# Token forms of later sequences made from untransposed rows in staging, and turned by transposing transfers

## Chip, cores and metric

The kernel runs on one core of one Trainium2 chip. The metric is the device time of the whole kernel in microseconds. Before the change it is 2253.17 us, the median of 3 runs (2252.21 to 2253.98).

## The reference

The input x holds 8 sequences of 1024 tokens with 512 features. With LN a layer norm without scale, the reference computes

```
x = x + attn(LN(x))        # per sequence: latent projections, causal softmax over 1024 tokens, head size 64
h = silu(y @ W1.T) * (y @ W3.T)          # y = LN(x), W1 and W3 are 2048 x 512
x = x + (fwht(h) / sqrt(2048)) @ W2.T    # Walsh-Hadamard transform of h, W2 is 512 x 2048
```

The two products with W1 and W3 need y with its features on the partitions; the layer norm gives y with its tokens on them. So y must be turned somewhere. What changes is how it is turned, and when.

## The kernel before, in words

**The work.** A block k (`NK` = 128 of them) is one group of 128 hidden rows (h = k mod 16) of one sequence (s = k // 16). It has seven products with f16 operands, `product(k, i)` for i = 0 to 6 (line 782), in a fast scheme with 7 block products in place of 8: each is 2 x 3 matmuls of 128x512 (lines 772 to 774; high*high, high*low, low*high parts). Their results stand in the four PSUM banks `PF`. Behind products 1, 3, 5 and 6 stands `down` (lines 796 to 798), six matmuls each, which multiplies earlier blocks' hidden values by W2. A block so has 66 matmuls of 128x512.

**The tokens' forms.** `XF` holds the right operands of the seven products: 7 forms, each a high and a low f16 part of 128x1024. Some forms are quarters of the tokens' matrix y^T (in `XS`, f32), some are sums that `tokens_sum` (VectorE, line 1721) writes over quarters in `XS`. `tokens_high` (ScalarE, line 1122) rounds a form to f16 into `XF`, and `tokens_low` (VectorE, line 1711) writes the rest. Form i of the next sequence can only be written once product i of the last block of this one (h = 15) has read the old form.

**The attention of the next sequence beside it.** While sequence s is in its blocks, the attention of sequence s+1 is computed in two halves of 512 tokens (a = 2s+2 and 2s+3). Its steps hang on slots: the position f = 7h + i, with i the product, gives slot f - 3 for the first half (f - 4 when s = 0) and 42 less (`ODD`) for the second; `slots` computes it, and there were 59 (`NSLOT`). Each engine walks the same positions in its own program order, in `fill(k, i)` on ScalarE and VectorE, so one table by hand sets the order in every queue. Where an engine reaches position f early or late relative to TensorE depends on its own queue. At the end of a half VectorE does `norm2` and `norm2_root` and then `xnorm` for four tiles (line 1533): it writes a normalised 128x512 tile into the one buffer `xs`. TensorE turns it (`xtrans`, line 616: four f32 transposes of 128x128 into the PSUM half `Y`), and ScalarE copies `Y` into `XS` (line 1003).

**ScalarE's and VectorE's part in a block.** After product 0 ScalarE's `copy_b` (line 1129) copies one PSUM bank to another, and product 2 waits for it. `copy_b` itself stands behind `high(k - 1)` (line 1148) in ScalarE's queue, which waits for VectorE's `hidden(k - 1, 0)` (line 1743). After product 2 VectorE's `sum_c` (line 1729) gives the bank that product 4 waits for. ScalarE's `silu` (line 1140) follows products 3 and 5; VectorE's `hidden(k, 1)` follows the second, then `out_rows` (line 1762). At the change of a sequence the steps of the forms stand between these.

**Transfers.** All are issued by SyncE, in program order: the weights' forms `WS` for two blocks ahead (896 KB, line 408), W2 (line 419), x and xT, the output, and, in the attention, the transposing transfers of the probabilities `PT<-Ph` and `PT<-Pl` (line 431; f16, in 128x128 blocks, up to 8 blocks each).

Of the kernel before, what the change touches and what calls it, by code (L numbers as in the profile page):

```python
# [9 lines left out]
F16 = mybir.dt.float16  # L10
# [7 lines left out]
NS = 8  # L18
# [26 lines left out]
NSLOT = 59  # L45
# [56 lines left out]
def xf_no(s, i):  # L102

    return 7 * s + ((0, 2, 4, 1, 3, 5, 6)[i] if s == 0 else i) + 1

# [31 lines left out]
def build_kernel(nc, x, xT, w13, w13t, w2, small, cst, tab, wscr, w2scr, w2tmp, out):  # L137
    with ExitStack() as ctx:
# [149 lines left out]
        def xblock(i):  # L288

            half, k = XPLACE[i]  # L290
            return XS[:, half, 2 * k:2 * k + 2, :].rearrange("p k c -> p (k c)")
# [16 lines left out]
        d_raw, d_PT = sem("d_raw"), sem("d_PT")  # L308
        d_wst, d_wld, d_w2st, d_w2ld = ([sem(f"{m}{i}") for i in range(2)] for m in ("d_wst", "d_wld", "d_w2st", "d_w2ld"))
# [31 lines left out]
        def _(sp):  # L341
# [140 lines left out]
            for k in range(NK):  # L482
                s, h = divmod(k, NH)
                for j in range(7):
                    if s + 1 < NS:
                        for c, slot in slots(s, 7 * h + j):
                            attention(2 * s + 2 + c, slot)
                    if s and j == 0 and 1 <= h <= 4:
# [25 lines left out]
        def _(pe):  # L514
# [96 lines left out]
            def xtrans(a, t):  # L611
                nonlocal yfree
                w.wait_ge(v_xs, tile_no(a, t))
                w.wait_ge(*yfree)
                for j in range(4):
                    i = pe.transpose(Y[:, j * 128:(j + 1) * 128], xs[:, j * 128:(j + 1) * 128], idn)  # L616
                i.then_inc(p_xt, 1)
                yfree = (a_xn, tile_no(a, t))

            def attention(a, slot):  # L620
                if 1 <= slot <= 4:
                    cproj(a, slot - 1)
                if slot == 6:
                    latent(a)
                if slot == 13:
                    values(a)
                if slot == 14:
                    proj(a)
                for t in range(4):
                    at = slot - tile_slot(a, t)  # L630
# [6 lines left out]
                    if slot == end_slot(a) + 5 + t:  # L637
                        xtrans(a, t)
# [106 lines left out]
            def product(k, i):  # L745
# [4 lines left out]
                if h == 0:  # L750
# [176 lines left out]
        def _(ac):  # L927
# [18 lines left out]
            def latent(a):  # L946
                w.wait_ge(p_cp, tile_no(a, 3))
                if a > 1:
                    w.wait_ge(v_pl, group_no(a - 1, 3, groups(a - 1) - 1))
                ac.activation(work(a)[2], banks(a)[0], ACT.Copy).then_inc(a_cT, 1)  # L950
# [48 lines left out]
            def xtrans(a, t):  # L999
                w.wait_ge(p_xt, tile_no(a, t))  # L1000
                if a >= 2:
                    w.wait_ge(v_xf, 7 * (a // 2))
                ac.activation(XS[:, a % 2, :, t * 128:(t + 1) * 128], Y.rearrange("p (j c) -> p j c", j=4), ACT.Copy).then_inc(a_xn, 1)

            def attention(a, slot):
# [11 lines left out]
                for t in range(4):  # L1017
# [5 lines left out]
                    if slot == end_slot(a) + 5 + t:  # L1023
                        xtrans(a, t)
# [86 lines left out]
            def tokens_high(s, i):  # L1111
                if i in (0, 3):
                    w.wait_ge(a_xn, tile_no(2 * s, 3))
                elif i == 5:
                    w.wait_ge(a_xn, tile_no(2 * s + 1, 3))
                else:
                    w.wait_ge(v_t, 4 * s + {1: 1, 4: 2, 2: 3, 6: 4}[i])
                if s:
                    w.wait_ge(p_gu, gu_no(NH * s - 1, i))
                else:  # L1120
                    w.wait_ge(a_nm, 2 * NH)
                ac.activation(XF[:, 0, i, :], xblock(i), ACT.Copy).then_inc(a_xf, 1)
# [166 lines left out]
            def fill(k, j):  # L1289
# [7 lines left out]
                if s == 0 and f in SPLIT_AT:  # L1297
                    split2(SPLIT_AT[f])

            for k in range(NK):  # L1300
                s, h = divmod(k, NH)
                first, last = s > 0 and h == 0, s + 1 < NS and h == NH - 1
# [9 lines left out]
                if first:  # L1312
                    tokens_high(s, 3)
                if last:
                    tokens_high(s + 1, 0)
# [4 lines left out]
                if first:  # L1320
                    tokens_high(s, 4)
# [3 lines left out]
                if last:  # L1325
                    tokens_high(s + 1, 1)
                fill(k, 2)
                if first:
                    tokens_high(s, 5)
# [4 lines left out]
                if first:  # L1334
                    tokens_high(s, 6)
                fill(k, 4)
                silu(k, 1)
                if last:
                    tokens_high(s + 1, 2)
# [7 lines left out]
        def _(ve):  # L1347
# [166 lines left out]
            def norm2(a):  # L1514
                sv.after(kept["x2"])
                if a == 1:
                    w.wait_ge(v_xs, 4)
# [12 lines left out]
            def xnorm(a, t):  # L1530
                sv.after(kept["norm2"])
                w.wait_ge(p_xt, tile_no(a, t) - 1)
                ve.tensor_scalar(xs[:, :], xrow(a, t), st[:, 184 + 2 * t:185 + 2 * t], st[:, 84 + t:85 + t],  # L1533
# [4 lines left out]
            def attention(a, slot):  # L1538
# [25 lines left out]
                for t in range(4):  # L1564
# [9 lines left out]
                    if slot == end_slot(a) + 4 + t:  # L1574
# [134 lines left out]
            def tokens_low(s, i):  # L1709
                w.wait_ge(a_xf, xf_no(s, i))  # L1710
                ve.tensor_tensor(XF[:, 1, i, :], xblock(i), XF[:, 0, i, :], ALU.subtract).then_inc(v_xf, 1)

            def tokens_sum(s, i):

                w.wait_ge(a_xn, tile_no(2 * s + 1, 3))
# [3 lines left out]
                b12, b22 = (XS[:, 1, 2 * j:2 * j + 2, :].rearrange("p k c -> p (k c)") for j in range(2))  # L1719
                u, v = {1: (b12, xblock(0)), 4: (b22, b12), 2: (b22, xblock(1)), 6: (xblock(3), xblock(2))}[i]  # L1720
                ve.tensor_tensor(xblock(i), u, v, ALU.subtract).then_inc(v_t, 1)
# [168 lines left out]
            def fill(k, j):  # L1890
# [5 lines left out]
                if s == 0:  # L1896
# [5 lines left out]
                    if f in SPLIT_AT:  # L1902
                        split2(SPLIT_AT[f])

            for k in range(NK):
                s, h = divmod(k, NH)
                first, last = s > 0 and h == 0, s + 1 < NS and h == NH - 1
# [5 lines left out]
                if first:  # L1913
                    tokens_low(s, 3)
                    tokens_low(s, 4)
                fill(k, 0)
                if last:
                    tokens_low(s + 1, 0)
                    tokens_sum(s + 1, 1)
# [8 lines left out]
                if first:  # L1928
                    tokens_low(s, 5)
                    tokens_sum(s, 6)  # L1930
                if last:
                    tokens_low(s + 1, 1)
                    tokens_sum(s + 1, 4)
# [3 lines left out]
                if k == 0 or first:  # L1937
                    tokens_low(s, 6)
                if last:
                    tokens_sum(s + 1, 2)  # L1940
# [3 lines left out]
                if last:  # L1944
                    tokens_low(s + 1, 2)
# [129 lines left out]
```

## Time and profile before

| | |
|---|---|
| median of 3 runs | 2253.17 us |
| the profiled execution's own time | 2254.15 us |
| its span (first to last instruction) | 2252.3 us |
| mean granted TensorE clock | 0.983 of full speed |
| TensorE matmul busy | 2143.6 us (95%) |
| VectorE, ScalarE, GpSimd busy | 64%, 44%, 10% of the span |

In the profile a matmul's record is longer than its share of the array, because matmuls overlap: one of 128x512 is recorded with 0.38 us while the next starts 0.216 us after it. So the distance between starts tells what an instruction costs TensorE. "Idle before" counts from the recorded end, and is 0.16 us less than what the array lost.

### The profile page before, as it was taken

To read this page: it belongs to the slowest core of one execution; us is meant where nothing else is said; L and a number is where in the kernel's file an instruction comes from. 1 tells how busy PE (TensorE), PEld (TensorE's weight loads), DVE (VectorE), ACT (ScalarE), POOL (GpSimd) and SP (SyncE) were. 2 spreads that over 40 slices of the span, in tenths; PEclk is the share of its full clock that TensorE was granted. 3 is DMA by queue.
4 is the path that set the end of the run, shared out by engine and by line. 5 is a ranking of instruction groups with operands and counts; after the bars stand their busy time and mean duration, and the time that the engine had idled before them with its cause. 6 is when DMAs were issued, how large, how long until landed. Compare 5 with 4: busy or idle time off the path is not lost. (4 is left out here: it accounts for less than half of the span.)

```text
span 2252.3 us, 27382 instructions
## 1 busy us (share of the span) xinstructions
PE 2143.6 (95%) x10108; PEld 1012.6 (45%) x10108; DVE 1448.9 (64%) x2758; ACT 982.7 (44%) x1493; POOL 234.1 (10%) x212
## 2 busy tenths in 40 slices
PE   6778899999999999999999999999999999999999
PEld 3433444444444444444444444444444444444444
DVE  7886676767657675666757675576756667563333
ACT  6855454434443534434444444435344344442221
POOL 2344554000000000000000000000000000000000
PEclk8789999999999999999999999999999999999999
DMA  8344324333233323234233332333332342323221
GB/s 330 138 146 156 123 93 130 122 108 103 91 97 120 120 101 99 88 114 140 74 107 116 116 98 87 102 115 121 100 99 94 111 137 74 105 82 112 84 85 54
DMA packets 127654, 252.97 MB, mean 112 GB/s; under 512 B 74528, under 2 KB 74656, under 8 KB 122144
## 3 DMA queue, kind: packets, MB, share of 16 engines
q1 hardware_dynamic: 127520, 251.21, 33.7%
q8 instruction: 81, 1.33, 0.2%
q14 instruction: 53, 0.43, 0.1%
HBM read 194.81 MB, written 39.85 MB: 104 GB/s over the span
## 5 line engine op out<-in xcount | busy, mean ns | idle before, releaser
L772 PE MATMUL PF<-XF,WS 128*128 128x512 f16 x1792 | 685.4, 382 | 17.8 <-ACT PF L1129 10.0
L773 PE MATMUL PF<-XF,WS 128*128 128x512 f16 x1792 | 683.1, 381 | 0.0
L774 PE MATMUL PF<-XF,WS 128*128 128x512 f16 x1792 | 682.8, 381 | 0.0
L796 PE MATMUL PD<-W2S,H 128*128 128x512 f16 x1024 | 388.6, 379 | 0.0
L797 PE MATMUL PD<-W2S,H 128*128 128x512 f16 x1024 | 388.6, 379 | 0.0
L798 PE MATMUL PD<-W2S,H 128*128 128x512 f16 x1024 | 388.6, 379 | 0.0
L1140 ACT ACTIVATE SH<-PF,afs 128x512 f32<-128x512 f32 x256 | 175.8, 687 | 378.6 <-PE PF L774 377.8
L772 PEld LDWEIGHTS PF<-XF,WS 128*128 128x128 f16 x1792 | 176.1, 98 | 245.9 <-issue 39.1
L1743 DVE SCALAR_TENSOR_TENSOR SH<-PF,afs,SH 128x512 f32<-128x512 f32 x256 | 191.8, 749 | 140.3 <-ACT SH L1140 118.1
L1148 ACT ACTIVATE H<-SH 128x1024 f16<-128x1024 f32 x128 | 135.2, 1056 | 323.9 <-DVE SH L1743 323.9
L774 PEld LDWEIGHTS PF<-XF,WS 128*128 128x128 f16 x1792 | 176.2, 98 | 214.1 <-issue 4.7
L773 PEld LDWEIGHTS PF<-XF,WS 128*128 128x128 f16 x1792 | 176.4, 98 | 179.2 <-issue 8.0
L1751 DVE TENSOR_TENSOR H<-SH,H 128x1024 f16<-128x1024 f32 x128 | 156.8, 1225 | 130.3 <-ACT H L1148 130.1
L1762 DVE SCALAR_TENSOR_TENSOR ring<-PD,afs,ring 128x512 f32<-128x512 f32 x224 | 166.8, 745 | 52.5 <-PE PD L798 52.0
L1964 POOL TENSOR_TENSOR ring<-ring,bb 128x512 f32<-128x512 f32 x56 | 70.9, 1289 | 1231.6 <-DVE st L1388 1211.7
L1733 DVE TENSOR_TENSOR PF<-PF,p 128x512 f32<-128x512 f32 x128 | 89.1, 696 | 130.6 <-PE PF L774 129.7
L796 PEld LDWEIGHTS PD<-W2S,H 128*128 128x128 f16 x1024 | 100.3, 98 | 121.2 <-issue 0.6
L798 PEld LDWEIGHTS PD<-W2S,H 128*128 128x128 f16 x1024 | 100.3, 98 | 121.2 <-issue 0.6
L797 PEld LDWEIGHTS PD<-W2S,H 128*128 128x128 f16 x1024 | 100.3, 98 | 121.1 <-issue 0.6
L1729 DVE TENSOR_TENSOR PF<-PF,p 128x512 f32<-128x512 f32 x128 | 88.8, 693 | 20.0 <-PE PF L774 18.5
L1134 ACT ACTIVATE p<-PF 128x512 f32<-128x512 f32 x128 | 75.1, 587 | 36.9 <-PE PF L774 36.9
L1129 ACT ACTIVATE PF<-PF 128x512 f32<-128x512 f32 x128 | 74.4, 581 | 26.4 <-PE PF L774 26.4
(310 smaller groups left out, 2195.8 us busy)
## 6 DMA issues: line engine op xcount, KB each, us to landing
WS<-wscr SPq DMA_DIRECT2D x112, 896.0 KB, 4.7
W2S<-w2scr SPq DMA_DIRECT2D x30, 1024.0 KB, 4.8
xraw<-xT SPq DMA_DIRECT2D x58, 256.0 KB, 3.5
ring<-x SPq DMA_DIRECT2D x56, 256.0 KB, 4.3
wscr<-WS SPq DMA_DIRECT2D x16, 896.0 KB, 4.2
out<-ring SPq DMA_DIRECT2D x56, 256.0 KB, 2.9
XF<-w SPq DMA_DIRECT2D x16, 512.0 KB, 7.5
RAW<-w13t SPq DMA_DIRECT2D x16, 512.0 KB, 4.1
```

The costliest lines, as they stand in the source:

```text
L772: pe.matmul(bank, wh, th, start=i < 2 and j == 0, stop=False, skip_group_check=True)
L773: pe.matmul(bank, wh, tl, start=False, stop=False, skip_group_check=True)
L774: m = pe.matmul(bank, wl, th, start=False, stop=j == 1, skip_group_check=True)
L796: pe.matmul(PD[:, t % 2, :], th, wh, start=j == 0, stop=False)
L797: pe.matmul(PD[:, t % 2, :], th, wl, start=False, stop=False)
L798: m = pe.matmul(PD[:, t % 2, :], tl, wh, start=False, stop=j == 3)
L1140: ac.activation(SH[:, i, :], PF[:, (1 - k % 2, 2)[i], :], ACT.Silu, scale=afs[:, k % NH:k % NH + 1]).then_inc((a_sb, a_sc2)[i], 1)
L1148: ac.activation(H[:, q % 2, k % 4, 0, :], SH[:, :, :].rearrange("p i c -> p (i c)"), ACT.Copy).then_inc(a_hi, 1)
L1733: ve.tensor_tensor(PF[:, 3, :], PF[:, k % 2, :], p5[:, :], ALU.add).then_inc(v_e, 1)
L1743: ve.scalar_tensor_tensor(SH[:, i, :], PF[:, (k % 2, 3)[i], :], afs[:, 16 + h:17 + h], SH[:, i, :], ALU.mult, ALU.mult).then_inc((v_hA, v_ ...
L1751: ve.tensor_tensor(H[:, q % 2, k % 4, 1, :], SH[:, :, :].rearrange("p i c -> p (i c)"), H[:, q % 2, k % 4, 0, :], ALU.subtract).then_inc(v ...
L1762: ve.scalar_tensor_tensor(row, PD[:, t % 2, :], afs[:, 65:66], row, ALU.mult, ALU.add).then_inc(v_ev, 1)
```

## The change

From the second sequence on, `xnorm` writes its rows straight into `XS`, tokens on the partitions, one slot earlier. Sums and the f16 split work on these rows as they lie. The split goes to staging: three pairs of buffers in turn (form i uses pair i mod 3), which the attention has done with by then, `Ph`/`Pl`, `PT` and `PB`. SyncE's new `load_form` turns each part with one transposing transfer of 8 blocks into `XF`: 14 of them per sequence. TensorE's `xtrans`, ScalarE's copy out of `Y`, and the slots for them are gone. The forms' steps now have positions of their own, f = 96 to 111 of sequence s and 0 to 2 of the next. Within a form the columns now lie as (tile, half, 128) in place of (half, tile, 128), so that a matmul's moving operand is four pieces of 128 columns, 256 columns apart. The first sequence keeps its transposes and takes the new layout.

```
-NSLOT = 59
+NSLOT = 57
+def xload_no(s, i):
+    return 32 * ((3, 2, 2)[i % 3] * (s - 1) + i // 3 + 1)
...
+        def staging(i, m):
+            return ((Ph[:, :], Pl[:, :]), (PT[:, 0, :], PT[:, 1, :]),
+                    tuple(PB[:, h * 512:(h + 1) * 512].bitcast(F16) for h in range(2)))[i % 3][m]
...
+            def load_form(s, i):
+                w.wait_ge(p_gu, gu_no(NH * s - 1, i))
+                w.wait_ge(a_xf, xf_no(s, i))
+                for m in range(2):
+                    if m:
+                        w.wait_ge(v_xf, xf_no(s, i))
+                    sp.dma_start_transpose(XF[:, m, i, :].rearrange("p (b c) -> p b c", c=128), staging(i, m)).then_inc(d_XF[i % 3], 16)
...
# SyncE, s + 1 < NS: load_form(s + 1, i) at f == 105, 106, 108, 110, 111 for i = 0 to 4
# SyncE, s > 0:      load_form(s, 5) at f == 0, load_form(s, 6) at f == 2
...
# TensorE: def xtrans and its call are removed; product(k, i) with h == 0:
+                if h == 0 and s == 0:
                     w.wait_ge(v_xf, xf_no(s, i))
+                elif h == 0:
+                    w.wait_ge(d_XF[i % 3], xload_no(s, i))
-                    th, tl = (XF[:, m, i, j * 512:(j + 1) * 512] for m in range(2))
+                    th, tl = (XF[:, m, i, :].rearrange("p (t f c) -> p t f c", t=4, f=2)[:, j] for m in range(2))
...
# ScalarE: def xtrans and its call are removed; latent(a) waits, for even a > 2, also for
+                    w.wait_ge(p_gu, gu_no(NH * (a // 2 - 1), 6))
# tokens_high(s, i), in place of the wait for product i of the last block:
+                elif i >= 3:
+                    w.wait_ge(d_XF[i % 3], xload_no(s, i - 3))
+                elif i == 0:
+                    w.wait_ge(d_PT, pt_no(2 * s + 1, 3))
+                elif i == 1:
+                    w.wait_ge(p_pv, group_no(2 * s + 1, 3, 1))
+                else:
+                    w.wait_ge(v_pl, group_no(2 * s + 1, 3, 1))
# ScalarE's positions, s + 1 < NS: tokens_high(s + 1, i) at f == 96, 103, 105, 108, 109, 111
#   for i = 0 to 5 (before: i = 0, 1, 2 at h == 15); s > 0: tokens_high(s, 6) at f == 1
#   (before: i = 3, 4, 5, 6 at h == 0)
...
# VectorE: norm2(a) waits for v_xs 4 * a; xnorm(a, t) at end_slot(a) + 3 + t (before + 4 + t):
-                w.wait_ge(p_xt, tile_no(a, t) - 1)
-                ve.tensor_scalar(xs[:, :], xrow(a, t), ...
+                w.wait_ge(v_xf, 7 * (a // 2))
+                ve.tensor_scalar(XS[:, a % 2, t, :], xrow(a, t), ...
# VectorE's positions, s + 1 < NS: f == 97 low 0; 102 sum 1; 103 sum 4; 104 low 1 and sum 2;
#   106 low 2; 109 low 3; 110 low 4 and sum 6; s > 0: f == 0 low 5; 2 low 6
#   (before: low 0, sum 1, low 1, sum 4, sum 2, low 2 at h == 15; low 3, low 4, low 5, sum 6, low 6 at h == 0)
```

The lines that begin with # sum up lines of the diff in words.

## Rows read from the trace of the kernel before

**Rows 1.** The page: busy time, and TensorE's granted clock in 40 slices.
```profile
PE 2143.6 (95%) x10108; PEld 1012.6 (45%) x10108; DVE 1448.9 (64%) x2758; ACT 982.7 (44%) x1493; POOL 234.1 (10%) x212
PEclk8789999999999999999999999999999999999999
```
**Rows 2.** Busy time per engine in two stretches: sequence 2's blocks, sequence 7's last ones.
```profile
688.00:949.80 261.80, 257.11 (x1242) 121.65 (x1241) 171.93 (x334) 113.86 (x167) 9.98 (x8) 1.00 0.33 106
1998.90:2241.00 242.10, 242.10 (x1123) 109.65 (x1122) 99.33 (x124) 62.62 (x85) 0.00 (x0) 1.00 0.26 88
```
**Rows 3.** Timeline, TensorE, second tile turned without a wait: start, recorded us, instruction.
```profile
549.48 0.38 PE L798 MATMUL PD<-W2S,H 128*128 128x512 f16 x1
549.69 0.60 PE L616 MATMUL XY<-cst_s,xs 128*128 128x128 f32 x4
550.13 0.38 PE L772 MATMUL PF<-XF,WS 128*128 128x512 f16 x1
```
**Rows 4.** Waits of TensorE from 426 to 1999 us: total, times, longest.
```profile
PE XY L616 <- DVE xs L1533: 4.7, 12, 0.6
```
**Rows 5.** Timeline, TensorE, position 4 of sequence 2: the first projection of the attention.
```profile
696.85 0.38 PE L774 MATMUL PF<-XF,WS 128*128 128x512 f16 x1
697.90 0.50 PE L529 MATMUL XY<-Kh,Wc 128*128 128x512 f32 x1 [0.68 <-DVE Kl L1383]
```
**Rows 6.** Timeline, VectorE, what stands ahead of that projection's low part.
```profile
694.90 1.22 DVE L1711 TENSOR_TENSOR XF<-XS,XF 128x1024 f16<-128x1024 f32 x1
696.03 1.22 DVE L1721 TENSOR_TENSOR XS<-XS 128x1024 f32<-128x1024 f32 x1
697.16 0.69 DVE L1383 TENSOR_TENSOR Kl<-xraw,Kh 128x512 fp32r<-128x512 f32 x1
```
**Rows 7.** Timeline, TensorE, the first sequence's blocks: two tiles turned after waits.
```profile
287.27 0.63 PE L616 MATMUL XY<-cst_s,xs 128*128 128x128 f32 x4 [1.43 <-ACT XS L1003]
...
402.06 0.66 PE L616 MATMUL XY<-cst_s,xs 128*128 128x128 f32 x4 [1.95 <-DVE xs L1533]
```
**Rows 8.** Groups by line and form: count, busy us, mean ns, idle before.
```profile
L1140 ACT ACTIVATE SH<-PF,afs 128x512 f32<-128x512 f32 x235 | 161.4, 687 | 350.7 <-PE PF L774 349.9
L1743 DVE SCALAR_TENSOR_TENSOR SH<-PF,afs,SH 128x512 f32<-128x512 f32 x236 | 176.8, 749 | 132.7 <-ACT SH L1140 111.9 <-PE PF L774 20.4
L1148 ACT ACTIVATE H<-SH 128x1024 f16<-128x1024 f32 x118 | 124.7, 1056 | 297.8 <-DVE SH L1743 297.8
L1762 DVE SCALAR_TENSOR_TENSOR ring<-PD,afs,ring 128x512 f32<-128x512 f32 x203 | 151.1, 744 | 33.1 <-PE PD L798 32.6
L1122 ACT ACTIVATE XF<-XS 128x1024 f16<-128x1024 f32 x49 | 50.8, 1052 | 25.5 <-DVE XS L1721 25.5
L1003 ACT ACTIVATE XS<-XY 128x512 f32<-128x512 f32 x52 | 30.9, 595 | 62.1 <-PE XY L616 62.1
```
**Rows 9.** Timeline around block 30 (h = 14): ScalarE's `copy_b`, then TensorE's product 2.
```profile
660.82 0.58 ACT L1129 ACTIVATE PF<-PF 128x512 f32<-128x512 f32 x1
...
661.64 0.38 PE L772 MATMUL PF<-XF,WS 128*128 128x512 f16 x1
```
**Rows 10.** Transfers by issue: count, median us to landing; one late issue of 8 blocks; landing range.
```profile
PT<-Ph SPq DMA_TRANSPOSE x56, 2.7
PT<-Pl SPq DMA_TRANSPOSE x56, 2.6
...
906.52 1.33 SPq L431 DMA_TRANSPOSE PT<-Pl  x1
...
DMA to landing us min/median/max: 2.3/2.6/4.5
```
**Rows 11.** Timeline, TensorE: eight f16 matmuls of 128 columns, and the next product.
```profile
531.13 0.61 PE L597 MATMUL XY<-PT,V 128*128 128x128 f16 x8
531.58 0.38 PE L772 MATMUL PF<-XF,WS 128*128 128x512 f16 x1
```

More of the change, by code:

```diff
@@ L286, in xrow, with xquarter, xblock, xpart @@
             return ring[:, r, :] if r < 16 else WX[:, t * 512:(t + 1) * 512]
-        def xblock(i):
-            half, k = XPLACE[i]
-            return XS[:, half, 2 * k:2 * k + 2, :].rearrange("p k c -> p (k c)")
+        def xquarter(s, half, k):
+            if s == 0:
+                return XS[:, half, 2 * k:2 * k + 2, :].rearrange("p f (t c) -> p f t c", t=4)
+            return XS[:, half, :, k * 256:(k + 1) * 256]
+        def xblock(s, i):
+            return xquarter(s, *XPLACE[i])
+        def xpart(s, i, m):
+            if s == 0:
+                return XF[:, m, i, :].rearrange("p (t f c) -> p f t c", t=4, f=2)
+            return staging(i, m).rearrange("p (t c) -> p t c", t=4)
+        def staging(i, m):
+            return ((Ph[:, :], Pl[:, :]), (PT[:, 0, :], PT[:, 1, :]),
+                    tuple(PB[:, h * 512:(h + 1) * 512].bitcast(F16) for h in range(2)))[i % 3][m]
         def parts_taken(a, t):
@@ L308, in build_kernel @@
         d_raw, d_PT = sem("d_raw"), sem("d_PT")
+        d_XF = [sem(f"d_XF{i}") for i in range(3)]
         d_wst, d_wld, d_w2st, d_w2ld = ([sem(f"{m}{i}") for i in range(2)] for m in ("d_wst", "d_wld", "d_w2st", "d_w2ld"))
@@ L487, in _ @@
                             attention(2 * s + 2 + c, slot)
+                    f = 7 * h + j
+                    if s + 1 < NS:
+                        if f == 105:
+                            load_form(s + 1, 0)
+                        if f == 106:
+                            load_form(s + 1, 1)
+                        if f == 108:
+                            load_form(s + 1, 2)
+                        if f == 110:
+                            load_form(s + 1, 3)
+                        if f == 111:
+                            load_form(s + 1, 4)
+                    if s:
+                        if f == 0:
+                            load_form(s, 5)
+                        if f == 2:
+                            load_form(s, 6)
                     if s and j == 0 and 1 <= h <= 4:
@@ L609, in outp @@
                 yfree = (v_x2, tile_no(a, t))
[L611 to L618, printed above, removed]
             def attention(a, slot):
@@ L636, in attention @@
                         outp(a, t)
-                    if slot == end_slot(a) + 5 + t:
-                        xtrans(a, t)
             def scores1(a, t):
@@ L770, in product @@
                     wh, wl = (WS[:, k % 2, m, WFORM[i], j * 128:(j + 1) * 128] for m in range(2))
-                    th, tl = (XF[:, m, i, j * 512:(j + 1) * 512] for m in range(2))
+                    th, tl = (XF[:, m, i, :].rearrange("p (t f c) -> p f t c", t=4, f=2)[:, j] for m in range(2))
                     pe.matmul(bank, wh, th, start=i < 2 and j == 0, stop=False, skip_group_check=True)
@@ L949, in latent @@
                     w.wait_ge(v_pl, group_no(a - 1, 3, groups(a - 1) - 1))
+                if a > 2 and a % 2 == 0:
+                    w.wait_ge(p_gu, gu_no(NH * (a // 2 - 1), 6))
                 ac.activation(work(a)[2], banks(a)[0], ACT.Copy).then_inc(a_cT, 1)
@@ L997, in parts_o @@
                 ac.activation(l[0:64, :], h[0:64, :].bitcast(F32), ACT.Copy).then_inc(a_ol, 1)
[L999 to L1003, printed above, removed]
             def attention(a, slot):
@@ L1022, in attention @@
                         parts_o(a, t, oh, ol)
-                    if slot == end_slot(a) + 5 + t:
-                        xtrans(a, t)
             def norms(h, i):
@@ L1111, in tokens_high @@
             def tokens_high(s, i):
+                rows = v_xs if s else a_xn
                 if i in (0, 3):
-                    w.wait_ge(a_xn, tile_no(2 * s, 3))
+                    w.wait_ge(rows, tile_no(2 * s, 3))
                 elif i == 5:
-                    w.wait_ge(a_xn, tile_no(2 * s + 1, 3))
+                    w.wait_ge(rows, tile_no(2 * s + 1, 3))
                 else:
                     w.wait_ge(v_t, 4 * s + {1: 1, 4: 2, 2: 3, 6: 4}[i])
-                if s:
-                    w.wait_ge(p_gu, gu_no(NH * s - 1, i))
-                else:
-                    w.wait_ge(a_nm, 2 * NH)
-                ac.activation(XF[:, 0, i, :], xblock(i), ACT.Copy).then_inc(a_xf, 1)
+                if s == 0:
+                    w.wait_ge(a_nm, 2 * NH)
+                elif i >= 3:
[4 more added lines that the diff above has]
+                    w.wait_ge(p_pv, group_no(2 * s + 1, 3, 1))
+                else:
+                    w.wait_ge(v_pl, group_no(2 * s + 1, 3, 1))
+                ac.activation(xpart(s, i, 0), xblock(s, i), ACT.Copy).then_inc(a_xf, 1)
             def copy_b(k):
@@ L1298, in fill @@
                     split2(SPLIT_AT[f])
+                if s + 1 < NS:
+                    if f == 96:
+                        tokens_high(s + 1, 0)
+                    if f == 103:
+                        tokens_high(s + 1, 1)
+                    if f == 105:
+                        tokens_high(s + 1, 2)
+                    if f == 108:
+                        tokens_high(s + 1, 3)
+                    if f == 109:
+                        tokens_high(s + 1, 4)
+                    if f == 111:
+                        tokens_high(s + 1, 5)
+                if s and f == 1:
+                    tokens_high(s, 6)
             for k in range(NK):
                 s, h = divmod(k, NH)
-                first, last = s > 0 and h == 0, s + 1 < NS and h == NH - 1
                 split = s == 0 and 1 <= h < NH - 1
@@ L1311, in _ @@
                         tokens_high(0, i)
[L1312 to L1315, printed above, removed]
                 if split:
@@ L1319, in _ @@
                 copy_p5(k)
-                if first:
-                    tokens_high(s, 4)
                 if split:
@@ L1324, in _ @@
                 fill(k, 1)
-                if last:
-                    tokens_high(s + 1, 1)
                 fill(k, 2)
-                if first:
-                    tokens_high(s, 5)
                 silu(k, 0)
@@ L1333, in _ @@
                 fill(k, 3)
-                if first:
-                    tokens_high(s, 6)
                 fill(k, 4)
                 silu(k, 1)
-                if last:
-                    tokens_high(s + 1, 2)
                 fill(k, 5)
@@ L1515, in norm2 @@
                 sv.after(kept["x2"])
-                if a == 1:
-                    w.wait_ge(v_xs, 4)
+                if a:
+                    w.wait_ge(v_xs, 4 * a)
                 for t in range(4):
@@ L1531, in xnorm @@
                 sv.after(kept["norm2"])
-                w.wait_ge(p_xt, tile_no(a, t) - 1)
-                ve.tensor_scalar(xs[:, :], xrow(a, t), st[:, 184 + 2 * t:185 + 2 * t], st[:, 84 + t:85 + t],
+                w.wait_ge(v_xf, 7 * (a // 2))
+                ve.tensor_scalar(XS[:, a % 2, t, :], xrow(a, t), st[:, 184 + 2 * t:185 + 2 * t], st[:, 84 + t:85 + t],
                                  ALU.subtract, ALU.mult).then_inc(v_xs, 1)
@@ L1573, in attention @@
                         parts_o(a, t, X[:, 0:128], oh, ol)
-                    if slot == end_slot(a) + 4 + t:
+                    if slot == end_slot(a) + 3 + t:
                         xnorm(a, t)
@@ L1710, in tokens_low @@
                 w.wait_ge(a_xf, xf_no(s, i))
-                ve.tensor_tensor(XF[:, 1, i, :], xblock(i), XF[:, 0, i, :], ALU.subtract).then_inc(v_xf, 1)
+                ve.tensor_tensor(xpart(s, i, 1), xblock(s, i), xpart(s, i, 0), ALU.subtract).then_inc(v_xf, 1)
             def tokens_sum(s, i):
-                w.wait_ge(a_xn, tile_no(2 * s + 1, 3))
+                w.wait_ge(v_xs if s else a_xn, tile_no(2 * s + 1, 3))
                 w.wait_ge(v_t, 4 * s + {1: 0, 4: 1, 2: 2, 6: 3}[i])
                 w.wait_ge(v_xf, xf_no(s, {1: 0, 4: 0, 2: 1, 6: 3}[i]))
-                b12, b22 = (XS[:, 1, 2 * j:2 * j + 2, :].rearrange("p k c -> p (k c)") for j in range(2))
-                u, v = {1: (b12, xblock(0)), 4: (b22, b12), 2: (b22, xblock(1)), 6: (xblock(3), xblock(2))}[i]
-                ve.tensor_tensor(xblock(i), u, v, ALU.subtract).then_inc(v_t, 1)
+                b12, b22 = xquarter(s, 1, 0), xquarter(s, 1, 1)
+                u, v = {1: (b12, xblock(s, 0)), 4: (b22, b12), 2: (b22, xblock(s, 1)), 6: (xblock(s, 3), xblock(s, 2))}[i]
+                ve.tensor_tensor(xblock(s, i), u, v, ALU.subtract).then_inc(v_t, 1)
             def sum_c(k):
@@ L1903, in fill @@
                         split2(SPLIT_AT[f])
+                if s + 1 < NS:
+                    if f == 97:
+                        tokens_low(s + 1, 0)
+                    if f == 102:
+                        tokens_sum(s + 1, 1)
+                    if f == 103:
+                        tokens_sum(s + 1, 4)
+                    if f == 104:
+                        tokens_low(s + 1, 1)
+                        tokens_sum(s + 1, 2)
+                    if f == 106:
+                        tokens_low(s + 1, 2)
+                    if f == 109:
+                        tokens_low(s + 1, 3)
+                    if f == 110:
+                        tokens_low(s + 1, 4)
+                        tokens_sum(s + 1, 6)
+                if s:
+                    if f == 0:
+                        tokens_low(s, 5)
+                    if f == 2:
+                        tokens_low(s, 6)
             for k in range(NK):
                 s, h = divmod(k, NH)
-                first, last = s > 0 and h == 0, s + 1 < NS and h == NH - 1
                 if k:
@@ L1912, in _ @@
                     low_part(k - 1)
-                if first:
-                    tokens_low(s, 3)
-                    tokens_low(s, 4)
                 fill(k, 0)
-                if last:
-                    tokens_low(s + 1, 0)
-                    tokens_sum(s + 1, 1)
                 fill(k, 1)
@@ L1927, in _ @@
                     tokens_sum(0, 6)
[L1928 to L1933, printed above, removed]
                 fill(k, 2)
@@ L1936, in _ @@
                 sum_e(k)
-                if k == 0 or first:
+                if k == 0:
                     tokens_low(s, 6)
-                if last:
-                    tokens_sum(s + 1, 2)
                 fill(k, 4)
@@ L1943, in _ @@
                 out_rows(k // 4 - 1, 2 * (k % 4))
-                if last:
-                    tokens_low(s + 1, 2)
                 fill(k, 5)
```

1 line of the change is left out of this document (removed).

## The prediction

> **What bounds the kernel now.** I read the page first. TensorE is recorded busy for 95% of the span, and from the third slice of 40 on its granted clock is near full (2.4 GHz) [rows 1]. Then two stretches: in a sequence with attention beside it (261.8 us) TensorE is busy for 257.1, VectorE for 172, ScalarE for 114; in the last sequence, without attention, TensorE is busy without a gap [rows 2]. So TensorE's queue is the bound, and a change is worth what it takes from or adds to that queue: instructions at their distance from start to start, and gaps. VectorE and ScalarE count only where they are late for TensorE. Third, the waits tell which gaps belong to what is removed [rows 4 to 7].
>
> **The change part by part.** Seven sequences get new forms this way, 14 halves of four tiles: 56 groups of four f32 transposes.
>
> *Removed, TensorE's transposes.* Between two products a group takes the place from 549.69 to 550.13: 0.44 us [rows 3]. 56 x 0.44 = **24.6 us**, all of it in the queue that binds.
>
> *Removed, the waits ahead of them.* `xs` is a single buffer: VectorE can write the next tile only when the last is turned. In the sequences 1 to 6 TensorE waits 12 times for it, 4.7 us recorded [rows 4], and 0.16 us more each time, since a record outlasts its share of the array (0.38 against 0.22): 4.7 + 12 x 0.16 = **6.6 us**. In the first sequence there are two larger ones, 1.43 and 1.95 recorded [rows 7]. The first waits for ScalarE's copy out of `Y`, which goes: 1.6 us. The second stands where VectorE is late with everything, and whoever waits for it next (product 4, for `sum_c`, ahead of which a form's low part and two tiles now stand) loses about as much. I take **1.6** of both, with 0 and 5 as ends.
>
> *Removed, ScalarE's copies.* 56 x 0.595 = 33 us [rows 8], off TensorE's path, taken at nothing: ScalarE is busy for 44%. If its cover went, it would be a gain.
>
> *Moved, the forms' steps.* Their number and size are as before. Ahead of the first projection at position 4, VectorE now works through five forms' steps after the change of sequence (low 3, 4, 5, sum 6, low 6), the last two before the low part of xT for which TensorE waits [rows 6]; the gap is 697.90 - 696.85 - 0.22 = 0.83 us [rows 5]. After the change only low 5 and low 6 stand there, two operations of 1.22 in place of four or five, so this gap goes: 6 x 0.83 = **5.0 us** (the seventh change of sequence is followed by no attention).
>
> They move to the last three blocks, and there they delay `copy_b`, for which product 2 waits. Three places, by the durations of [rows 8]:
> - End of h = 13: low 0 (1.22; its successor starts 1.14 later [rows 6]) stands ahead of `hidden`, behind which stand `high` and `copy_b` on ScalarE. `copy_b` ends at 661.40 now, and product 2 starts at 661.64 [rows 9]: 0.24 of slack, so 0.9 us of new gap.
> - End of h = 14: after the second silu VectorE does `hidden` 0.75, `out_rows` 0.74, sum 4, low 1 and sum 2 (1.22 each, [rows 6, 8]), `hidden` 0.75; then ScalarE `high` 1.06 and `copy_b` 0.58. That is 7.54, plus silu's 0.69 and some 0.2 to start it, less about 0.5 since VectorE's operations overlap by 0.08: 7.9 us after the end of product 5. TensorE reaches the next product 2 after six groups of six matmuls, 36 x 0.216 = 7.8. New gap some 0.3.
> - End of h = 15: the same with low 4 and sum 6 only, but `tokens_high` 5 (1.05) ahead of `copy_b`: 7.4 + 0.9 - 0.4 = 7.9. New gap some 0.3.
>
> Together 1.5 us, seven times: **10.5 us** given back. Ends: 0 (the gaps merge, since each one gives VectorE time) and 3 us each, 21, if starts and semaphores add up.
>
> *Added, 98 transposing transfers* (14 x 7), on SyncE's queue. The trace has 112 of their kind. A late one of 8 blocks, the same 256 KB, holds SyncE 1.33 us; to landing it is 2.3 to 4.5 us from the issue [rows 10]. Two of a pair are issued 1.3 us apart and each lands 2.6 or 2.7 after its own issue, so they overlap. Per sequence SyncE spends 14 x 1.3 = 18 us on them, in a stretch of some 25. The tightest is form 5: its low part ends after hidden, `high`, low_part and itself, some 6.2 us after product 6 of h = 15; issue and landing (3 to 4) make 9 to 10; product 5 of the new sequence starts eight groups of six (10.4), the last gap (0.3) and a projection (0.6) later, at about 11.3. Slack 1 us or more, so nothing. Form 6 has 2 us, forms 0 to 4 more. Behind these transfers stand, on SyncE, the weights for h = 1 (1.5 us later, needed 14 us on), W2 (needed four blocks on), and xT: hidden. If a landing took 2 us more, form 5 would be late by 1.
>
> *Added waits.* ScalarE's for the staging buffers: forms 3 and 4 need loads 0 and 1, issued behind products 0 and 1, 4 us and more earlier; behind them in the queue stand the second silu and `copy_b`. `latent`'s wait is for a product three positions back. VectorE's `norm2` waits for its own past work. Nothing for each; GpSimd's queue is not touched.
>
> *Changed, the moving operand.* All 5376 matmuls of products now read four pieces of 128 columns. No row shows such an operand. Lower end 0; upper end: each piece as dear as a matmul of its own, 0.45 us for eight [rows 11], 0.056 each, 4 x 0.056 - 0.216 = 8 ns, or 45 us. I take 0, since the nearest row is the product's own matmul of 512 columns, of which only the addresses change, while the upper end counts four instructions where there is one. The Trainium skill (SBUF — State Buffer, "Door 1: The DMA port swizzle", the note on "cachelines") ties the penalty for a stride to how many accesses in a row fall into one 16-byte line. Within a piece the elements stay dense, so by it the cost would be 0; no run here shows it.
>
> **Sum.** 24.6 + 6.6 + 1.6 + 5.0 - 10.5 = 27.3. From the profiled execution's 2254.15 that is 2226.9; the median of the runs is 1 us below that execution, so **2226 us**. With the terms' ends: 24.6 + 6.6 + 5 + 5.0 = 41 at best (2212), 24.6 + 6.6 + 0 - 21 = 10 at worst (2243).
>
> **The rivals.**
> 1. *Strided operand dear.* Place: every product's matmul; price up to 8 ns each, 45 us. The time would be 2226 + 45 = 2271, slower. It decides from 27.3 / 5376 = 5 ns on. Against it: the operand's data are as dense within a piece as before. Chance 0.04.
> 2. *Forms land late.* Rows as above say no. But take the parts one after another, each with its 3.2 us to landing: 14 x 3.2 = 45 us from the end of product 0 of h = 15, where the need of the last is some 27 us on. Then 18 us of gap per change of sequence, 7 x 18 = 126, about 2352. The Trainium skill (VectorE: DVE Perf Modes, "The three transpose paths" and "Rules for kernel authors") speaks against this change: it gives 390 ns for a 128x128 transpose on TensorE and 1309 ns for one by DMA, and says to use TensorE where a PSUM destination is fine. By its figure 14 x 8 x 1.3 would be an estimated 147 us per sequence, far more. The trace disagrees, with 8 blocks issued in 1.33 us and landed within 4.5 [rows 10]. A partial lateness of 4 us at each change would cancel the gain. Chance 0.06.
> 3. *Only the exchange of waits differs.* `copy_b`'s gaps stay away, and the gain is the removed terms: 36 to 41 us, 2212 to 2217. For it: 90 us of idle VectorE time in a sequence [rows 2]. Chance 0.18.
> 4. *The chain behind `copy_b` grows*, 3 us or more per change, with the gap at position 4 still there: 5 to 14 us gained, 2239 to 2248. Chance 0.12.
> 5. *Nothing to be seen.* The transposes filled time that other waits take over. Against it: 42 of 56 groups have no wait ahead of them. Chance 0.04.
>
> **How the numbers follow.** The forecast, 2218 to 2238, has 0.56. A measurement of this kernel can tell 0.2% (4.5 us) from no change. Faster by more: the forecast, rival 3, rival 4: 0.86; within: rival 5, 0.04; slower: rivals 1 and 2, 0.10. The range takes in the forecast, rival 3 and the nearer part of rival 4: 2212 to 2241.
>
> **What would show it.** No L616 and no ScalarE copy out of `XY` after the first blocks; a sequence 3.5 us shorter for the transposes, with the `xs` waits gone. At h = 14, h = 15 and the next h = 0, gaps of product 2 on `copy_b` of 0.3 to 0.9 us. At position 4 no gap. XF<-staging transfers landing 2.5 to 4.5 us after issue, and no wait of TensorE on them. The distance of product matmuls still 0.216. The forecast is wrong if that distance grows, if TensorE waits for `XF` transfers, or if ScalarE waits for them and `copy_b` behind it.

## The result, and the profile after

The changed kernel takes 2260.3 us (median of 7 runs, 2257.8 to 2261.96) against 2253.17 us before (7 runs): ratio 1.0032, 95% interval 1.002 to 1.0043. It is slower by 7 us, where 27 us less were forecast. The profiled execution's span went from 2252.3 to 2259.3 us.

The page of the kernel after:

```profile
span 2259.3 us, 26978 instructions
PE 2132.1 (94%) x9884; PEld 986.5 (44%) x9884; DVE 1449.7 (64%) x2758; ACT 948.6 (42%) x1437; POOL 233.7 (10%) x212
PEclk8789999999999999999999999999999999999999
```

The 224 transposes are gone (10108 matmuls before [rows 1], 9884 now), and ScalarE has 34 us less to do. VectorE's work is as it was. So the removal is real, and the gain went elsewhere. Busy time in stretches of the kernel after, the first being sequence 3's blocks:

```profile
954.60:1215.60 261.00, 253.95 (x1209) 117.70 (x1208) 171.90 (x334) 108.98 (x159) 9.97 (x8) 1.00 0.41 120
1069.70:1085.30 15.60, 15.40 (x73) 7.16 (x73) 13.49 (x35) 4.93 (x8) 3.60 (x3) 1.00 0.22 83
1085.30:1102.50 17.20, 15.84 (x76) 7.21 (x75) 13.34 (x32) 5.29 (x8) 1.38 (x2) 1.00 0.32 115
```

A sequence takes 261.0 us against 261.8 [rows 2]: a gain of 0.8 where some 4 were forecast. TensorE's busy time fell by 3 us, but the idle time rose. And this sequence is one of the better ones. Both kernels have one wait of 0.47 us for `copy_b` late in each sequence; from one of these to the next it is 264.0, 261.1, 262.1, 266.7 and 261.1 us now, and was 261.8, 261.8, 262.7, 262.7 and 261.9. Who ended its gaps, from 428 to 2005 us:

```profile
PE PF L811 <- ACT PF L1170: 15.5, 30, 0.8
PE XY L577 <- DVE Kl L1424: 13.3, 18, 2.7
PE XY L601 <- DVE V L1473: 9.1, 12, 1.1
PE XY L645 <- DMA PT<-Pl: 8.9, 14, 2.5
PE PF L811 <- DVE PF L1771: 1.2, 6, 0.2
```

The first row is `copy_b` (7.5 us in 12 waits before, 15.5 in 30 now). Of the 18 new waits the prediction had 12, two at each of six changes of sequence (0.76 and 0.28); the other six, of 0.28, stand at position 57 of each sequence. No row names the forms' transfers. But the projections of an attention (L577) wait 13.3 us in place of 6.7, and up to 2.7 in place of 0.7, and `values` (L601) 9.1 in place of 2.5, with six new waits of 1.1. The prediction had neither growth. TensorE's timeline at both, and at the two larger `copy_b` gaps:

```profile
969.72 0.38 PE L837 MATMUL PD<-W2S,H 128*128 128x512 f16 x1
971.47 0.50 PE L577 MATMUL XY<-Kh,Wc 128*128 128x512 f32 x1 [1.38 <-DVE Kl L1424]
...
1090.76 0.38 PE L813 MATMUL PF<-XF,WS 128*128 128x512 f16 x1
1092.23 0.40 PE L601 MATMUL XY<-id,V 128*128 128x128 f16 x4 [1.09 <-DVE V L1473]
1092.47 0.38 PE L811 MATMUL PF<-XF,WS 128*128 128x512 f16 x1
1092.68 0.38 PE L812 MATMUL PF<-XF,WS 128*128 128x512 f16 x1
...
1190.56 0.39 PE L811 MATMUL PF<-XF,WS 128*128 128x512 f16 x1 [0.76 <-ACT PF L1170]
...
1205.26 0.39 PE L811 MATMUL PF<-XF,WS 128*128 128x512 f16 x1 [0.28 <-ACT PF L1170]
```

With the 0.16 that a record hides, the gap ahead of the projection is 1.54 us here, of `values` 1.25 and of `copy_b` 0.92 and 0.44. Product matmuls follow at 0.21 to 0.22 us as before, so the strided operand costs nothing. (The slice in the kernel is `rearrange("p (t f c) -> p f t c", t=4, f=2)[:, j]`: half j of all four tiles. The cut of the code under "The change" has `p t f c` there, which would take tile j.)

**Where xT is late.** SyncE's timeline of the kernel after, at the start of sequence 4, and then the issues of that stretch (count, KB, median us to landing):

```profile
1219.07 2.68 SPq L463 DMA_TRANSPOSE XF<-PB  x2
1221.79 1.40 SPq L463 DMA_TRANSPOSE XF<-Ph  x1
1223.23 1.34 SPq L463 DMA_TRANSPOSE XF<-Pl  x1
1224.62 0.58 SPq L441 DMA_DIRECT2D W2S<-w2scr  x1
1225.24 1.46 SPq L385 DMA_DIRECT2D xraw<-xT  x2
1226.74 2.13 SPq L380 DMA_DIRECT2D WX<-x  x4
...
W2S<-w2scr SPq DMA_DIRECT2D x1, 1024.0 KB, 5.4
xraw<-xT SPq DMA_DIRECT2D x2, 256.0 KB, 5.6
```

Before, W2 was issued 5.8 us ahead of xT and had landed by then:

```profile
1215.61 0.32 SPq L419 DMA_DIRECT2D W2S<-w2scr  x1
1221.41 2.68 SPq L363 DMA_DIRECT2D xraw<-xT  x2
```

SyncE now comes to W2's place in its program only behind `load_form` 5 and 6, which wait for VectorE. So 1 MB goes out 0.6 us ahead of xT, for which the next projections wait. In the kernel before the first xT load of a sequence landed 2.8 or 2.9 us after its issue; now the two loads behind W2 take 5.6 to 6.5 us (the median of the two, in each of the six sequences). Over all the loads that their line issues the median went from 3.5 to 5.1: minimum, median and maximum of line 385 after and of line 363 before are

```profile
DMA to landing us min/median/max: 2.9/5.1/8.1
```

```profile
DMA to landing us min/median/max: 2.8/3.5/7.8
```

The gaps behind it differ per sequence (1.5 to 2.9 us), and in two of the six TensorE's clock falls: behind those recorded with 2.69 and 1.93 us, but not behind one of 2.28. The largest:

```profile
705.74 0.38 PE L837 MATMUL PD<-W2S,H 128*128 128x512 f16 x1
708.80 0.50 PE L577 MATMUL XY<-Kh,Wc 128*128 128x512 f32 x1 [2.69 <-DVE Kl L1424]
...
712.45 0.63 PE L812 MATMUL PF<-XF,WS 128*128 128x512 f16 x1
712.88 0.63 PE L813 MATMUL PF<-XF,WS 128*128 128x512 f16 x1
```

After the gap matmuls follow at 0.43 us, the lower of the two levels (1.2 GHz), for some 3 us, which costs 1.7 more. Read off the timeline in this way, the six sequences lose about 15 us to xT: 11.9 in gaps, and twice 1.7 to the clock.

**Where VectorE is the bound.** The two blocks h = 7 and 8 together took 34.0 us before and take 32.8 now:

```profile
802.30:820.90 18.60, 17.62 (x90) 8.86 (x90) 15.14 (x40) 6.72 (x11) 4.99 (x4) 1.00 0.21 77
820.90:836.30 15.40, 15.40 (x77) 7.34 (x75) 11.54 (x27) 5.78 (x9) 0.00 (x0) 1.00 0.32 116
```

These are the rows of before, to be held against the second and third stretch after. The first block lost 3.0 us, as forecast (four groups of 0.44 and 1.1 of waits), but VectorE's work of both blocks stayed at some 26.8 us. It has hardly a gap there. Its busy time (the third engine in the row) is 17.1 of the 18.0 us from position 52 to 58 after, and was 17.0 of 19.1 before:

```profile
1074.20:1092.20 18.00, 16.67 (x79) 7.46 (x77) 17.14 (x52) 4.17 (x7) 4.99 (x4) 1.00 0.23 81
806.80:825.90 19.10, 18.32 (x95) 9.22 (x92) 16.98 (x52) 6.40 (x11) 4.99 (x4) 1.00 0.14 49
```

At position 58 TensorE needs `values`' operand, at the end of VectorE's chain for the second half (`norm1`), and it waits for `copy_b` at 57: 1.7 us come back.

### The profile page after: what moved, and what is told of

Same layout as the page of the kernel before. It is cut to its first block and busy times, and to the rows that moved or that the text cites. A ratio compares the mean times of both kernels' runs of the same rounds, so it can differ in the third digit from the quotient of the medians.

```text
span 2259.3 us, 26978 instructions
## 1 busy us (share of the span) xinstructions
PE 2132.1 (94%) x9884; PEld 986.5 (44%) x9884; DVE 1449.7 (64%) x2758; ACT 948.6 (42%) x1437; POOL 233.7 (10%) x212
```

## The experiments

The ratios are against the kernel before, measured beside each on the same chip (2252.6 to 2253.5 us). Gains over the kernel after are against its 2260.3 us, a difference of two medians.

**W2 one block later.** In the kernel after:

```
-                    if j == 2 and k % 4 == 0 and k >= 8:
+                    if k >= 8 and j == 2 and (k % NH == 1 if k % NH < 4 else k % 4 == 0):
                         load_w2s(k // 4)
```

> The kernel after, with the W2 load of a sequence's first block issued one block later (at h = 1 in place of h = 0), so that it no longer stands just ahead of the first xT loads on SyncE's queue. Theory A (the xT transfers for positions 3 and 4 land late because the 1 MB of W2 now runs ahead of them): the gap of TensorE ahead of the projection at position 7 (1.5 to 2.9 us and up to 1.7 us of half clock, 13.6 us in sequences 1 to 6) goes, xT lands 3 to 4 us after its issue again, and the time is 2246 to 2249 us, against 2260 after. Rival B (the transposing transfers themselves are what xT waits behind): xT still lands 5 us or more after its issue, the gap stays, 2258 to 2261.

Measured 2243.59 us, ratio 0.9956 (0.9942 to 0.9971). The median is 16.7 us below the kernel after, 2.4 us more than theory A's band allows. This one issue decides between slower and faster than before. TensorE's waits of this kernel, 427 to 1988 us, and its transfers:

```profile
PE XY L577 <- DVE Kl L1424: 3.2, 14, 0.6
```

```profile
xraw<-xT SPq DMA_DIRECT2D x58, 256.0 KB, 3.8
```

13.3 us became 3.2. The loads into `xraw` land in 3.8 us at the median (4.9 after, 3.5 before), and W2, now behind them, is waited for by nobody. Rival B falls: the transposing transfers still go out right ahead of xT, yet a sequence's first xT load lands after 3.3 to 3.5 us in the four sequences where it can be read alone.

**Is it the order alone?** The first attempt moved W2 in the kernel before from behind position 2 to ahead of the xT loads.

> The kernel before, unchanged but for the issue of W2 in a sequence's first block, which moves from behind position 2 to just ahead of the xT loads of position 3. Theory A (the order alone makes xT late): xT lands 5 us or more after its issue, TensorE gets a gap ahead of the projection at position 6 or 7 of 1 us and more in each of 6 sequences, 2259 to 2264 us. Rival B (the transposing transfers' own traffic is needed for it): no such gap, 2252 to 2256.

Measured 2253.16 us, ratio 1.0002 (0.9992 to 1.0011). That says nothing on the question: SyncE waits for nothing between the two places, so W2 left 5.8 us ahead of xT, as before. The second attempt holds W2 back in time:

```
+                    if h == 0 and k >= 8 and j == 3:
+                        if s + 1 < NS:
+                            w.wait_ge(v_xl, tile_no(2 * s + 2, 0))
+                        load_w2s(k // 4)
```

> The previous run of this question (e8_before_w2_at_xt) moved the issue in the program but not in time, since SyncE waits for nothing between: W2 was still issued 5.8 us ahead of xT. Here the kernel before issues W2 of a sequence's first block only after the same wait as the xT load of position 3, so right ahead of it, with no transposing transfers near. Theory A (the order alone makes xT late): xT lands 5 us or more after its issue in place of 2.9, and TensorE gets a gap of 1 us and more ahead of the projection of position 6 or 7: 2259 to 2266 us. Rival B (the transposing transfers' traffic is needed too): xT lands within 4 us, 2252 to 2256.

Measured 2260.78 us, ratio 1.0034 (1.002 to 1.0047): the order alone, without one transposing transfer of forms, makes the kernel before 8 us slower. SyncE's timeline in it, the landing of both transfers, and the waits for the projections (426 to 1999 us):

```profile
961.60 0.32 SPq L419 DMA_DIRECT2D W2S<-w2scr  x1
961.97 2.32 SPq L363 DMA_DIRECT2D xraw<-xT  x2
```

```profile
W2S<-w2scr SPq DMA_DIRECT2D x1, 1024.0 KB, 4.8
xraw<-xT SPq DMA_DIRECT2D x1, 256.0 KB, 5.3
```

```profile
PE XY L533 <- DVE Kl L1387: 11.7, 24, 1.0
```

In the six sequences this first xT load lands 5.3 to 5.6 us after its issue, as theory A has it. Six gaps of 0.84 (recorded) came on top of the 18 before, 6.0 of the 8 us. They are smaller than in the kernel after, where x and the last forms are issued in the same few microseconds too; how much of the rest is those transfers was not tried.

**Transposes put back where VectorE is busy.** In the kernel after, at the first half's old places:

```
+            def turn_nothing(a, t):
+                w.wait_ge(*yfree)
+                for j in range(4):
+                    pe.transpose(Y[:, j * 128:(j + 1) * 128], idn, idn)
...
+                    if a % 2 == 0 and slot == end_slot(a) + 5 + t:
+                        turn_nothing(a, t)
```

> The kernel after, with four f32 transposes of the identity into Y put back at the four positions where the first half's tiles were turned (f = 52 to 55, 28 groups in all, 28 x 0.44 = 12.3 us of TensorE's time); nothing reads what they write. Theory A (VectorE, with no idle time from position 52 to 56, sets when TensorE may go on at position 57 and 58): they cost nothing or up to 2 us in all, the gap at position 57 and 58 (1.7 us per sequence) shrinks by what they take; 2258 to 2263 us. Rival B (TensorE's queue is the bound there): 12 us more, 2272.

Measured 2254.99 us, ratio 1.0011 (1.0002 to 1.0021). 12.3 us of TensorE's work more, and the kernel is 5 us faster. The wait of `values` is back at its 2.5 us (from 425 to 2003 us):

```profile
PE XY L601 <- DVE V L1480: 2.5, 6, 0.4
```

Theory A holds in its mechanism: in each of the sequences 1 to 6 the new waits of 1.09 and 0.28, 1.7 us with what the records hide, are gone, and the four groups take 1.8. Its time is 3 us too high. Part of that is in the first sequence: there block h = 8 of the kernel after has waits of 2.06 and 1.74 us and then runs at the lower clock, and with the transposes the first wait is 0.41 and the clock stays up. By the end of this sequence the variant is 2.6 us ahead. The two profiled executions differ by 2.2 us in all, the medians by 5; where the rest comes from is not shown. So in the kernel after, four transposes per tile of the first halves cost next to nothing.

**Transposes put back in the second half**, the same edit with `a % 2 and slot == end_slot(a) + 3 + t`.

> The kernel after, with four f32 transposes of the identity into Y put back at f = 98 to 101, the second half's tiles (28 groups, 12.3 us of TensorE's time). The kernel after has gaps there of 0.92 us at position 100 (product 2 of h = 14 waits for copy_b) and 0.45 at 107. Theory A (VectorE's chain behind copy_b sets the pace there too): the two groups ahead of position 100 fill the gap of 0.92, and those behind it the one of 0.45, so 1.75 - 1.37 = 0.4 us per sequence, 3 us in all: 2257 to 2265. Rival B (TensorE's queue alone): 12 us, 2272.

Measured 2263.49 us, ratio 1.0047 (1.0032 to 1.0062): 3.2 us more than after, for 12.3 us of work. At h = 14 TensorE is now late enough for `copy_b`: the waits for it go from 30 to 24 (427 to 2008 us).

```profile
PE PF L818 <- ACT PF L1177: 10.9, 24, 0.8
```

**Transposes taken away in the kernel before**, three quarters of each:

```
-                for j in range(4):
+                for j in range(1):
                     i = pe.transpose(Y[:, j * 128:(j + 1) * 128], xs[:, j * 128:(j + 1) * 128], idn)
...
-                ac.activation(XS[:, a % 2, :, t * 128:(t + 1) * 128], Y.rearrange("p (j c) -> p j c", j=4), ...
+                ac.activation(XS[:, a % 2, 0, t * 128:(t + 1) * 128], Y[:, 0:128], ...
```

> The kernel before, with only the first of the four transposes of each tile, and only its 128 columns copied out of Y: three quarters of the turned tokens of sequences 1 to 7 are left out. It takes 56 x 0.33 = 18.5 us off TensorE and nothing off VectorE. Theory A (only the second half's 28 groups stand where TensorE is the bound; the first half's time comes back as a gap at positions 52 to 58): 8 to 13 us less than before, 2240 to 2245. Rival B (what the prediction took, each group is worth its place in the queue): 18 us less, 2235 or below.

Measured 2241.96 us, ratio 0.995 (0.9935 to 0.9964): 11.5 us for 18.5 us of work, within theory A's 8 to 13. The waits of the transposes for `xs` grow where the work went (424 to 1988 us; 4.7 before [rows 4]). They are the third and fourth tile of each first half, and both waits grow by 0.33, which is what their own group gave up:

```profile
PE XY L616 <- DVE xs L1533: 8.6, 12, 0.9
```

These 3.9 us are part of the 7 that did not come; in the profiled execution one late landing of `PT<-Pl`, of which more below, is another. So in the kernel before, what two of the four groups of a first half take was covered by VectorE's lateness, not what all four take.

**VectorE relieved at 50 to 58.** In the kernel after, `NSLOT = 79`, and

```
-                    if slot == end_slot(a) + 3 + t:
+                    if slot == (end_slot(a) + 3 if a % 2 else 75) + t:
                         xnorm(a, t)
```

> The kernel after, with the first half's four normalised tiles (L1575) written at f = 78 to 81 instead of 50 to 53, where VectorE has idle time. Theory A (VectorE's queue at 50 to 58 is the bound): the gap at positions 57 and 58 goes in each sequence (1.7 x 6 = 10 us, and up to 5 us in the first), 2245 to 2250 us. Rival B (the gap hangs on another chain, such as the projections' waits): it stays, 2258 to 2261.

Measured 2251.24 us, ratio 0.9993 (0.9983 to 1.0002), 9 us below after, 1 short of the expected band, and not to be told from the kernel before. The same two blocks in this kernel:

```profile
1067.60:1083.30 15.70, 15.51 (x74) 7.08 (x73) 13.17 (x39) 4.92 (x8) 4.94 (x4) 1.00 0.23 87
1083.30:1098.70 15.40, 15.40 (x75) 7.35 (x74) 11.06 (x25) 5.46 (x8) 0.00 (x0) 1.00 0.35 128
```

31.1 us for both, where 34.0 - 2.9 = 31.1 was what the prediction would have.

**The first `copy_b` gap removed**: `tokens_low(s + 1, 0)` at f == 98 in place of 97.

> The kernel after with the low part of form 0 alone moved, from f = 97 to 98, behind hidden and low_part of h = 13. The first of the three gaps for copy_b that the prediction summed (0.9 us, 7 times) goes and nothing else changes: 2254 us, against 2260. If VectorE is as late anyway, 2258 to 2261.

Measured 2254.7 us, ratio 1.0012 (1.0003 to 1.0021): 5.6 us less than after, for 6.4 forecast.

**Together.** Three moves (W2, tiles, low 0), then a fourth:

> The kernel after with three moves: W2 one block later, the first half's tiles at f = 78 to 81, and the low part of form 0 at f = 98 in place of 97 (behind hidden and low_part). If the gaps are separate, their gains add: 16.7 (W2, measured) + 9 (tiles, measured) + 0.92 x 7 = 6.4 (the gap at position 100 of h = 14): 2260 - 32 = 2228 us. If one gap only uncovers the next, 2236 or more.

Measured 2231.24 us, ratio 0.9903 (0.9888 to 0.9918). The gains add, to within 3 us of 2228.

```
# the fourth, VectorE: low 1 and sum 2 at f == 105 (was 104), low 2 at 107 (106)
# ScalarE: high 2 at f == 106 (was 105)
```

> e7 with low 1 and sum 2 at f = 105 (behind hidden and low_part of h = 14) in place of 104, high 2 at 106 and low 2 at 107. The gap of 0.45 us that product 2 of h = 15 has for copy_b goes: 3 us less than e7, 2225. If sum_c, which then has two forms' steps ahead of it, comes late for product 4, there is a gap at position 109 instead and no gain.

Measured **2227.49 us**, ratio 0.9887 (0.9873 to 0.9902), 3.7 us below the three moves (3 were forecast), 1.1% faster than before and the fastest of all. A sequence in it, and its waits on `copy_b` (428 to 1971 us):

```profile
942.40:1198.70 256.30, 253.08 (x1210) 118.02 (x1209) 170.04 (x333) 109.34 (x159) 9.93 (x8) 1.00 0.42 122
```

```profile
PE PF L811 <- ACT PF L1170: 8.6, 13, 1.0
```

## Why the prediction was wrong

By its steps:

- *TensorE's transposes, 24.6 us, and the waits ahead of them, 6.6*: right as counted work, wrong as time for the **first halves**. "All of it in the queue that binds" was taken from averages over a sequence; rival 3, which named VectorE's 90 us of idle time, leaned on the same average. At positions 52 to 58 VectorE has hardly any (17.1 of 18.0 us busy). Of 2.9 us per sequence 1.7 came back, 10 us in six. The put-back transposes (free) and the relieved VectorE (9 us) show it; the quarter transposes (11.5 of 18.5) show the same in the kernel before, for half of a first half's groups.
- *The first sequence, 1.6 us and its four groups*: the blocks h = 7 and 8 there went from 42.6 to 44.6 us. The same shortage, dearer, since the longer gap ended in the lower clock (granted 0.89 over these blocks in place of 0.96). That is some 5.5 us off the forecast. The second wait of [rows 7], 1.95 us, came back as product 4's for `sum_c`, as said, but with 3.24.
- *The gap at position 4, 5.0 us*: it went, as said. VectorE was ahead there.
- **"W2 (needed four blocks on), and xT: hidden"**: this is the step that decided the sign. Each transfer behind the forms was asked for its own due time. What was not asked is in which order they now leave. W2 is in no hurry, but it went out just ahead of xT, which is. The term was put at nothing; it is some 15 us by the timeline, and 16.7 measured. Without it the other misses leave a gain of some 8 us, and with W2 moved the kernel is 9.6 us faster than before.
- *`copy_b`, 1.5 us per change*: right, also in its parts. 0.9, 0.3 and 0.3 were forecast; 0.92, 0.44 and, at the new h = 0, 0.16 came. Removing the first two in turn gave 5.6 and 3.7 us.
- *The forms' transfers*: right. They land 3.0 to 5.4 us after issue, at a median of 3.4 (2.5 to 4.5 forecast). Two of TensorE's weight loads wait 0.8 us for them in all, and ScalarE, for its staging buffers, 2.5 us in five places, where the prediction had nothing. The Trainium skill gives 1309 ns for one 128x128 block by DMA (VectorE: DVE Perf Modes, "The three transpose paths"); taken block by block, 8 would be an estimated 10.5 us by it. These do not go block by block: 8 land in 3.4 us.
- *The strided operand*: right, no cost. So rival 1 falls, and by the line above rival 2.
- One reading of [rows 1] was off by a slice: the granted clock is near full from the fourth slice on, not the third. And 5376 times 8 ns is 43 us, not 45 (rival 1). Nothing hangs on either.

The sum: 27.3 forecast, less 15 (xT), 10 (first halves), 5.5 (first sequence) and 3.5, is -6.7; the span grew by 7.0. The terms are read off one execution of each kernel, and that they meet so closely is in part luck. The 3.5 are one late landing of `PT<-Pl` in sequence 5, 1.8 us more than at this place before and 1.7 of lower clock behind it:

```profile
1572.94 0.51 PE L645 MATMUL XY<-PT,V 128*128 128x128 f16 x6 [2.46 <-DMA PT<-Pl]
```

It comes at the same place in some of the variants, with 2.1 us, and not in others. It also comes once, with 2.41 us and in sequence 3, in the kernel before with the quarter transposes, which has no transposing transfers of forms; so it does not need them. Its cause stays open.

Of the rivals, 5 (the transposes filled time that other waits take over) came nearest. It was priced at 0.04 because 42 of 56 groups had no wait ahead of them, but that shows only that the transposes were not late, not that the matmuls behind them would not be. It held for the first halves, and would alone have left a gain. The order of W2 and xT was in no rival: "slower" had 0.10, all of it from rivals 1 and 2, and neither came true.

## What to carry to other kernels

When a step with waits is put into an in-order queue, ask of what stands behind it not only whether it is still in time, but next to what it will now be issued: a large transfer that nobody needs soon can end up just ahead of a small one that everybody waits for. Before work is taken off the bound engine, look at the second busiest engine in that very stretch, not at its average: where it has no idle time, part or all of the work was free. And when a change loses, its parts may still be good: here four moves of lines in the order gave 33 us.

## What the runs showed of the hardware

- A 256 KB load issued 0.4 us behind a 1 MB load lands after 5.3 to 5.6 us instead of 2.9 (the kernel before with W2 held back); two of them issued 0.6 us and more behind it, after 5.6 to 6.5 (the kernel after).
- A moving operand in four pieces of 128 f16 columns, 512 bytes apart from start to start, runs at the pitch of a contiguous one: 0.21 to 0.22 us for 512 columns.
- A tiny VectorE operation can be held by GpSimd. In the first sequence a 128x4 product that takes 0.15 us elsewhere took 2.09, ending within 0.02 us of GpSimd's subtraction over 128x1024, in the kernel before as well as after. VectorE's and GpSimd's timelines of the kernel after:

```profile
288.04 2.09 DVE L1395 TENSOR_TENSOR st<-st 128x4 f32<-128x4 f32 x1
```

```profile
287.80 2.31 POOL L2042 TENSOR_TENSOR WS<-WX,WS 128x1024 f16<-128x1024 f32 x1 [1.51 <-ACT WS L1141]
```

The Trainium skill (SBUF — State Buffer, "SBUF: two separate sides") says of the port pair that VectorE and GpSimd share that the loser of the two is blocked for the whole instruction. The trace agrees, here with both inputs of each instruction in SBUF.
- TensorE's clock can fall behind a gap: in the kernel after some 3 us of matmuls 0.43 us apart (1.2 GHz) followed gaps recorded with 2.69, 2.46 and 1.93 us, and none followed one of 2.28.
